# Query, key and value projections as half-precision products of high and low parts

## The reference

```python
def attention(q, k, v, ...):                     # q = layernorm(x), k = v = ctx
    Q = (q @ Wq.T + bq).reshape(16, 256, 16, 32)
    K = (k @ Wk.T + bk).reshape(16, 256, 16, 32)
    V = (v @ Wv.T + bv).reshape(16, 256, 16, 32)
    score = einsum('bshd,bsgd->bshg', Q, K)
    weight = softmax(score, axis=-1)
    return einsum('bshg,bsgd->bshd', weight, V).reshape(16, 256, 512) @ Wo.T + bo
x = x + attention(layernorm(x), ctx, ctx, ...)
x = x + ffn(layernorm(x))    # 8 experts of width 352, two per token, and a shared expert of width 704
```

## Time and profile before

| what | us |
|---|---|
| median of 3 runs | 1515.64 (1507.03 to 1521.95) |
| the profiled execution | 1513.93 |
| its span in the trace | 1512.2 |
| TensorE busy, weight loads busy | 1403.4, 1069.2 |
| VectorE, ScalarE, GpSimd busy | 906.3, 647.3, 502.0 |
| chain that ended last: TensorE's share | 80% |

### The profile page before, as it was taken

One profiled execution on the slowest core, in us unless ns is written; L12 is line 12 of the kernel. 1 busy time (PEld: TensorE's weight loads), 2 busy tenths in 40 slices (PEclk: granted clock), 3 DMA queues, 4 the chain that ended last, 5 costly groups with the idle time before them and its releaser, 6 DMA issues.

```text
span 1512.2 us, 33003 instructions
## 1 busy us (share of the span) xinstructions
PE 1403.4 (93%) x10387; PEld 1069.2 (71%) x10388; DVE 906.3 (60%) x1984; ACT 647.3 (43%) x1500; POOL 502.0 (33%) x607
## 2 busy tenths in 40 slices
PE   4489999999999999679989999999999999999997
PEld 4388888888888888556657765666666666666675
DVE  6388888888888888766776552222222222223666
ACT  4256656555665556541145442333333333332221
POOL 4234444444444443200567101111111111114554
PEclk9699999999999999889999999999999999999999
DMA  5456677666766775838724332222222222226997
GB/s 188 95 120 174 182 170 188 173 173 176 176 175 175 180 176 134 291 125 323 154 43 69 100 99 98 83 83 83 83 83 83 81 81 81 83 77 191 313 303 238
DMA packets 261893, 223.20 MB, mean 148 GB/s; under 512 B 182997, under 2 KB 191261, under 8 KB 261486
## 3 DMA queue, kind: packets, MB, share of 16 engines
q1 hardware_dynamic: 244488, 179.41, 42.2%
q0 software_dynamic: 12880, 35.47, 7.9%
q10 hardware_dynamic: 4470, 7.61, 1.6%
HBM read 129.30 MB, written 67.96 MB: 130 GB/s over the span
## 4 chain that ended last, share of the span: by engine, by line
PE 80%; DVE 6%; ACT 4%; SPq 3%; issue 3%; DMA 3%; POOL 1%; another core or an unknown queue 0%; ACTq 0%; DVEq 0%; POOLq 0%
PE psum_b L716 41%; PE psum_a L716 32%; PE psum_b L1032 2%; SPq L486 2%; PE psum_a L813 2%; PE psum_b L1054 2%; ACT spread_t L1100 1%; SPq L661 1%; PE psum_b L742 1%; DMA base_rows<-base 1%; DVE wdn L1797 1%; DMA heads<-in_wk_t 1%; DVE gate_act L1686 1%; ACT z_parts L1136 1%; DVE d_m L1711 1%
## 5 line engine op out<-in xcount | busy, mean ns | idle before, releaser
L716 PE MATMUL psum_a<-wgu,zg_t 128*128 x1704 | 269.0, 315 | 1.9 <-DVE zg_t L1808 1.7
L1947 POOL TENSOR_TENSOR spread<-pr,own 128x512 f32<-128x512 f32 x128 | 136.7, 1099 | 317.6 <-DVE pr L1463 306.6
L716 PEld LDWEIGHTS psum_a<-wgu,zg_t 128*128 128x128 f16 x1704 | 166.4, 98 | 91.1 <-issue 10.1
L2021 POOL DMA_INDIRECT zg<-z_rows,gather_ix x71 | 67.2, 946 | 431.2 <-DVE gather_ix L1804 423.9
L716 PE MATMUL psum_a<-zt_in,wsgu 128*128 128x256 f16 x1536 | 174.8, 277 | 5.8 <-DMA base<-x_rows 2.8
L716 PEld LDWEIGHTS psum_a<-zt_in,wsgu 128*128 128x128 f16 x1536 | 151.0, 99 | 31.7 <-issue 8.1
L1813 DVE SCALAR_TENSOR_TENSOR silu<-psum_a,w_scale,silu 128x352 f32<-128x352 f32 x71 | 41.5, 584 | 195.0 <-ACT silu L1302 195.0
L716 PE MATMUL psum_b<-wdn,act_t 128*128 (+1 forms) x639 | 149.6, 379 | 1.6 <-DVE act_t L1820 1.6
L716 PE MATMUL psum_b<-wsdn,sh_t 128*128 128x512 f16 (+1 forms) x576 | 131.8, 382 | 16.8 <-DVE sh_t L1692 14.1
L1302 ACT ACTIVATE silu<-psum_a,w_scale 128x352 f32<-128x352 f32 x71 | 39.3, 553 | 203.8 <-PE psum_a L716 203.8
L716 PEld LDWEIGHTS psum_b<-wsdn,sh_t 128*128 128x128 f16 (+1 forms) x576 | 53.9, 98 | 88.9 <-issue 16.0
(11 more groups left out here) (245 smaller groups left out, 2509.7 us busy)
## 6 DMA issues: line engine op xcount, KB each, us to landing
expert_rows<-y_sb SPq DMA_DIRECT2D x71, 256.0 KB
k_st<-k_parts SPq DMA_DIRECT2D x192, 64.0 KB, 2.2
q_st<-q_parts SPq DMA_DIRECT2D x192, 64.0 KB, 2.1
wgu_in<-in_wgu_t SPq DMA_DIRECT2D x8, 1408.0 KB, 18.2
x_sb<-in_x SPq DMA_DIRECT2D x16, 512.0 KB, 3.4
cx_in<-in_ctx_t SPq DMA_DIRECT2D x16, 512.0 KB, 6.7
x_res<-in_x SPq DMA_DIRECT2D x16, 512.0 KB, 5.3
value_rows<-heads SPq DMA_DIRECT2D x16, 512.0 KB, 6.2
```

Of the source, the lines that this page charges most:

```text
L716: return nc.tensor.matmul(o, l, r, start=start, stop=stop)
L1947: G.tensor_tensor(spread[:, u * UG:(u + 1) * UG, :].rearrange("p r (g t) -> p r g t", t=GT), pr[:, s, u * UG:(u + 1) * UG, :].unsqueeze(3) ...
L2021: pool.indirect_dma_start(out=zg[:, b, :], out_offset=None, in_=z_d[:, :], in_offset=bass.IndirectOffsetOnAxis(ap=gather_ix[:, b:b + 1], a ...
```

## The change

The three projections take half-precision operands. As these have a narrow range, every operand gets a power of two: xn a fixed one (2 to the 11th), each weight matrix one from its largest magnitude (`weight_scale`), and each block of the context one from its own largest magnitude, which `key_scale` now works out beside the scale of the keys. The outputs are scaled back where they leave PSUM. For this

- a second buffer `cx_w` takes the context for `weigh_context`, one pass ahead of the one for the products; SP loads it with one more DMA per pass (`load_cw`);
- `key_scale` writes to `k_next` and stands after `normalise_x`; in its old place stand the two instructions of `take_key_scale`, which copy it to `k_scale`;
- `split_context` on GpSimd waits for the context's scale (`c_scaled`) and has one more instruction, which scales the block in place;
- at the start the largest values are found, turned and used in three phases (`LIMITS`), each for one weight matrix; the low parts of wq and wv go from GpSimd to VectorE; the masks of `q_st` and `k_st` are written first on ScalarE;
- the first moves of keys stand ahead of the load of the third context block on SP's queue, and the first moves of queries are issued by ScalarE.

The output projection stays as it was. The diff, cut to its core:

```diff
         cx_in = sb("cx_in", [P, KC, BT], F32, early)
-        cx_t = sb("cx_t", [P, 2, KC, BT], F32R, early)
+        cx_w = sb("cx_w", [P, KC, BT], F32, early)
+        cx_t = sb("cx_t", [P, 2, KC, BT], F16, early)
...
-        wq = sb("wq", [P, 2, KC, D], F32R, one)
-        wk = sb("wk", [P, 2, KC, D], F32R, one)
-        wv = sb("wv", [P, 2, KC, D], F32R, one)
+        wq = sb("wq", [P, 2, KC, D], F16, one)
+        wk = sb("wk", [P, 2, KC, D], F16, one)
+        wv = sb("wv", [P, 2, KC, D], F16, one)
+        below_wo = sb("below_wo", [P, 3, KC, D], F32, one)
...
+            def load_cw(i):
+                sp.dma_start(cx_w[:, :, :], cx_v[:, :, bass.ds(i * BT, BT)]).then_inc(cw_loaded, 16)
...
             load_w(wk_in, wk_t, wk_loaded)
+            load_cw(1)
...
-            sp.wait_ge(cx_weighed, 1)
+            sp.wait_ge(cx_weighed, 2)
             load_cx(1)
+            load_cw(2)
+            move_keys(-1)
             sp.wait_ge(xn_ready, 2 * SUB)
             load_x(2)
+            sp.wait_ge(cx_weighed, 3)
+            load_cw(3)
+            store_values(-1)
             sp.wait_ge(cx_split, 2)
-            sp.wait_ge(cx_weighed, 2)
             load_cx(2)
...
+                if ahead3 and ahead4:
+                    sp.wait_ge(cx_weighed, i + 4)
+                    settle(sp)
+                    load_cw(i + 4)
                 if ahead3:
-                    sp.wait_ge(cx_weighed, i + 3)
-                    settle(sp)
                     sp.wait_ge(cx_split, i + 3)
                     settle(sp)
                     load_cx(i + 3)
...
+            def turn_limits(phase):
+                pe.wait_ge(limits_ready, phase + 1)
+                for n in range(*LIMITS[phase]):
+                    at = phase * BANK + (n - LIMITS[phase][0]) * P
+                    last = nc.tensor.transpose(psum_a[:, at:at + P], limit_rep[:, n, :], ident[:, :])
+                last.then_inc(limits_turned, 1)
+            turn_limits(0)
+            turn_limits(1)
+            pe.wait_ge(wk_split, 2)
             project_k(-1, range(KC))
-            pe.wait_ge(limits_ready, 1)
-            for n in range(4):
-                last = nc.tensor.transpose(psum_a[:, n * P:(n + 1) * P], limit_rep[:, n, :], ident[:, :])
-            last.then_inc(limits_turned, 1)
+            turn_limits(2)
             pe.wait_ge(wq_split, 1)
...
+                    nc.scalar.activation(xn_t[:, HI, :, s * P:(s + 1) * P], bank_ap(f"X{s}").rearrange("p (c t) -> p c t", c=KC),
+                                         ACT.Copy, scale=2.0 ** Z_EXP).then_inc(xt_high, 1)
...
-            weights_high(wk, wk_in, wk_loaded, 16)
-            x_out(-1)
-            weights_high(wq, wq_in, wq_loaded, 16)
-            weights_high(wv, wv_in, wv_loaded, 16)
-            weights_high(wo, wo_in, wo_loaded, 32)
-            keys_out(-1, 0)
-            keys_out(-1, 1)
-            queries_out(-1, 0)
-            queries_out(-1, 1)
+            def scaled_high(n, w, w_in, loaded, chunks):
+                act.wait_ge(loaded, 16)
+                act.wait_ge(w_scaled, n + 1)
+                nc.scalar.activation(w[:, HI, chunks], w_in[:, chunks], ACT.Copy, scale=w_power[:, 3 + n:4 + n]).then_inc(w_high, 1)
             act.wait_ge(const_ready, 1)
             copy8 = [q_st[3 * HD:ROWS], k_st[3 * HD:ROWS]]
             for rows_below, factor, size in ((copy8[0], ident[0:GT, 0:GT], MASK_Q), (copy8[1], other[:, :], 1.0)):
                 nc.scalar.activation(rows_below.rearrange("p j (h t) q -> p (j h) t q", t=GT), factor.unsqueeze(1).unsqueeze(3).broadcast_to([GT, NJ * H, GT, GI]),
                                      ACT.Copy, scale=size).then_inc(mask_ready, 1)
+            x_out(-1)
+            scaled_high(0, wk, wk_in, wk_loaded, slice(0, KC // 2))
+            scaled_high(0, wk, wk_in, wk_loaded, slice(KC // 2, KC))
+            scaled_high(1, wq, wq_in, wq_loaded, slice(0, KC))
+            scaled_high(2, wv, wv_in, wv_loaded, slice(0, KC))
+            keys_out(-1, 0)
+            keys_out(-1, 1)
+            queries_out(-1, 0)
+            queries_out(-1, 1)
+            act.wait_ge(q_low, 2)
+            for n, part in enumerate(PARTS_OF_Q):
+                for l in range(4):
+                    act.dma_start(q_st[HD * n:HD * (n + 1), :, HD * l:HD * (l + 1), :].rearrange("p j m g -> p j (m g)"),
+                                  q_parts[HD * l:HD * (l + 1), part].rearrange("p j c t -> p j (c t)")).then_inc(q_moved, 16)
+            weights_high(wo, wo_in, wo_loaded, 32)
...
-                    V.tensor_tensor(v_rows[:, s], bank_ap(f"V{s}"), bv_rep[:, :], ALU.add).then_inc(drained[BANK_OF[f"V{s}"]], 1)
+                    V.scalar_tensor_tensor(out=v_rows[:, s], in0=bank_ap(f"V{s}"), scalar=k_scale[:, 8:9], in1=bv_rep[:, :],
+                                           op0=ALU.mult, op1=ALU.add).then_inc(drained[BANK_OF[f"V{s}"]], 1)
...
             def weigh_context(n):
-                dve.wait_ge(cx_loaded, n * 16 + 16)
-                link(V.tensor_reduce(out=k_scale[:, 7:8], in_=cx_in[:, :, :].rearrange("p c t -> p (c t)"), axis=X, op=ALU.max, apply_absolute_value=True))
+                if isinstance(n, int) and n == 0:
+                    dve.wait_ge(cx_loaded, 16)
+                else:
+                    dve.wait_ge(cw_loaded, n * 16)
+                whole_block = cx_in if isinstance(n, int) and n == 0 else cx_w
+                link(V.tensor_reduce(out=k_bound[:, 2:3], in_=whole_block[:, :, :].rearrange("p c t -> p (c t)"), axis=X, op=ALU.max, apply_absolute_value=True))
                 dve.sem_inc(cx_weighed, 1)
             def spread_context():
-                V.tensor_copy(c_rep[:, :], k_scale[:, 7:8].broadcast_to([P, P])).then_inc(c_rep_ready, 1)
-            def key_scale(first=False):
-                bits = lambda n: k_scale[:, n:n + 1].bitcast(U32)
-                link(V.tensor_scalar(k_scale[:, 0:1], k_scale[:, 0:1], k_scale[:, 5:6], k_scale[:, 6:7], ALU.mult, ALU.add))
-                link(V.tensor_scalar(bits(1), bits(0), EXPONENT, None, ALU.bitwise_and))
-                link(V.tensor_scalar(bits(1), bits(1), float(SMALLEST << 23), None, ALU.max))
-                link(V.tensor_scalar(bits(2), bits(1), -1.0, float((2 * 127 + K_ROOM) << 23), ALU.mult, ALU.add))
-                if not first:
-                    link(V.tensor_copy(k_scale[:, 3:4], k_scale[:, 4:5]))
-                link(V.tensor_scalar(k_scale[:, 4:5], k_scale[:, 1:2], q_scale[:, 3:4], None, ALU.mult))
-                V.tensor_scalar(k_scale[:, 8:8 + KC], bias_col[:, 1, :], k_scale[:, 2:3], None, ALU.mult).then_inc(k_scaled, 1)
+                V.tensor_copy(c_rep[:, :], k_bound[:, 2:3].broadcast_to([P, P])).then_inc(c_rep_ready, 1)
+            def key_scale():
+                powers, ups = (k_next[:, n:n + 2].bitcast(U32) for n in (2, 4))
+                link(V.tensor_scalar(k_next[:, 0:1], k_next[:, 1:2], k_bound[:, 0:1], k_bound[:, 1:2], ALU.mult, ALU.add))
+                link(V.tensor_scalar(powers, k_next[:, 0:2].bitcast(U32), EXPONENT, None, ALU.bitwise_and))
+                link(V.tensor_scalar(powers, powers, float(SMALLEST << 23), None, ALU.max))
+                link(V.tensor_scalar(ups, powers, -1.0, float((2 * 127 + K_ROOM) << 23), ALU.mult, ALU.add))
+                mark(V.tensor_scalar(k_next[:, 10:10 + KC], bias_col[:, 1, :], k_next[:, 4:5], None, ALU.mult))
+                link(V.tensor_scalar(k_next[:, 7:9], w_power[:, 6:8], k_next[:, 3:4], None, ALU.mult))
+                link(V.tensor_scalar(k_next[:, 9:10], k_next[:, 7:8], k_next[:, 4:5], None, ALU.mult))
+                dve.sem_inc(c_scaled, 1)
             def bound_out(i):
                 wait_full(dve, "M0", i)
-                V.tensor_reduce(out=k_scale[:, 0:1], in_=bank_ap("M0")[:, 0:P], axis=X, op=ALU.max).then_inc(drained[BANK_OF["M0"]], 1)
+                V.tensor_reduce(out=k_next[:, 1:2], in_=bank_ap("M0")[:, 0:P], axis=X, op=ALU.max).then_inc(drained[BANK_OF["M0"]], 1)
             def next_key_scale(i):
                 wait_drained(dve, "M0", i)
+                dve.wait_ge(cx_split, i + 3)
                 key_scale()
-            def first_scales():
+            def take_key_scale():
+                link(V.tensor_scalar(k_bound[:, 3:4], k_scale[:, 2:3], q_scale[:, 3:4], None, ALU.mult))
+                V.tensor_copy(k_scale[:, 2:10 + KC], k_next[:, 2:10 + KC]).then_inc(k_scaled, 1)
+            def limits_out(phase):
+                first, end = LIMITS[phase]
+                dve.wait_ge(limits_turned, phase + 1)
+                link(V.tensor_reduce(out=limits[:, first:end], in_=psum_a[:, phase * BANK:phase * BANK + (end - first) * P].rearrange("p (n c) -> p n c", c=P),
+                                     axis=X, op=ALU.max))
...
-            def body(i, behind, ahead, ahead2, weighs=0):
+            def body(i, behind, ahead, ahead2, weighs=0, ahead3=True):
                 bound_out(i - 1)
                 if behind:
```

(65 more changed lines are left out.)

99 lines of the change are left out of this document (58 added, 41 removed).

## The result

The changed kernel takes 1581.96 us, the median of four runs (1580.5 to 1585.19). The kernel before takes 1515.8 us on the same chip (four runs). The ratio is 1.0444, with a 95% interval from 1.0411 to 1.0478: slower. The profiled execution has a span of 1581.3 us and a mean granted clock of 0.957.

What follows compares the result with a forecast made beforehand. TensorE was taken as nearly full, with VectorE's string up to z right behind as second bound. 1513.9 + 78 (13 passes) - 10.5 (start) = 1581.4, plus 1.7 for the median: 1583 us; range 1505 to 1602, likeliest case 1562 to 1602.

Steps and rivals of the forecast that it cites:

- The products: TensorE's projections in each attention pass: half-precision operands save 1.2 us a pass, between nothing and 1.7 us.
- Rival (c): Half-precision products gain nothing, staying at 123 ns; VectorE sets the pass, so still 1583 us; no case of its own.
- Two-column instructions wait for GpSimd: VectorE's late key scale: its two- and four-column instructions wait out GpSimd's four weight-spreading products, 2.8 us more a pass.
- the 16 ns: Four-column VectorE instruction takes 230 ns, one-column 214; the difference was read as a sign that such instructions wait for GpSimd.
- z late beyond its 0.8 us: VectorE's late key scale adds about 1.5 us ahead of z, whose first half has 0.8 us in hand: 0.7 us a pass.
- z halves held by the split: Later z meets GpSimd's context split; each half loses up to one GpSimd instruction, 1.1 us a pass counted.
- The clock: TensorE, idle waiting for z, drops to 1.2 GHz; the transposes behind slow, about 1.4 us a pass (0 to 1.9).
- A steady pass: Sum for one attention pass: 6.0 us longer, between 4.5 and 7.2; over 13 passes +78 us (58 to 94).
- The start: Before the first scores: earlier key and query moves bring 9.5 us, pass 0 another 1 us: -10.5 us (-6 to -13).
- the 2.2 us of landing: At the start, the last query move on ScalarE's queue was taken to land 2.2 us after its issue.
- (a): Rival: two- and four-column instructions don't wait for GpSimd; 1529 us, without z meeting the split 1514; chance 0.30.
- (b): Rival, faster: VectorE's string isn't late at the transposes of z, so TensorE's 1.2 us come through; 1490 us; chance 0.10.

Runs made afterwards that it cites:

- before_one_wide: The kernel before, with three idle linked one-column VectorE instructions added between the normalisation of x and the residual sums: 1525.99 us, ratio 1.0125.
- before_two_wide: The kernel before, with three idle linked two-column VectorE instructions added between the normalisation of x and the residual sums: 1582.56 us, ratio 1.0486.
- key_early: The changed kernel with the key scale calculation moved back to its old place, right behind `take_key_scale`: 1518.7 us, ratio 1.008 to the kernel before.
- key_after_values: The changed kernel with the key scale calculation moved behind VectorE's value step, after z: 1508.7 us, ratio 1.0011 to the kernel before.
- no_pool_scale: The changed kernel without GpSimd's instruction that scales the context (not the same computation): 1597.47 us, ratio 1.0627 to the kernel before.
- loads_held: The changed kernel with SP's next loads at the start held until the first 12 query moves have landed: 1573.01 us, ratio 1.0453 to the kernel before.
- key_single: The changed kernel with the late key scale worked out in 14 one-column instructions instead of 7, same place: 1557.16 us, ratio 1.0323 to the kernel before.

## Why the prediction was right

The time (1583 against 1582) and the sign came out, and the mechanism did too: before_one_wide and before_two_wide show that the two-column instructions wait for GpSimd's products, key_early and key_after_values that the calculation's place makes the loss. The match to 1 us is luck: two errors of some 7 us cancelled.

- **The products.** Priced at 1.2 us a pass (0 to 1.7). The step from pass 13 to pass 14, without the late key scale, is 1.37 us shorter than before: right. The parts: keys and queries take 10.6 us for 96 products instead of 12.0, from start to next start, 1.4 less; the value product 0.37 less by its record; and each group of four scores now takes 0.46 us to the next start (311.90 to 312.36) against 0.39, some 0.4 us a pass given back, which wasn't foreseen. Rival (c) is out.
- **Two-column instructions wait for GpSimd, +2.8 us.** Measured: 4.1 us for the calculation instead of the 1.5 reckoned without the wait, 2.6 us. The prediction let mask, mask, complement and bias go one per GpSimd instruction; it was the three on two columns, and the bias on four came when GpSimd was through, so no run shows whether four columns wait. That the 16 ns were read as a sign of the waiting form was an inference from thin evidence; before_one_wide and before_two_wide make it good for two columns. The Trainium skill's rule (SBUF — State Buffer, "Who interferes with whom") fits these three instructions; z beside GpSimd's scaling was not blocked to that instruction's end (0.73 us for a half, of a scaling of 2.86).
- **z late beyond its 0.8 us, +0.7 us.** The start of z moves by 4.69 us in the pass (35.27 us from the attention sums before it, against 30.58). That is 4.14 for the calculation, 0.66 for the normalisation of x, and 0.1 regained earlier. The 0.66 wasn't foreseen: the normalisation takes 1.82 us, not 1.16, since GpSimd's products now begin beside it. Of the 0.8 us in hand only 0.65 could be used, as TensorE starts 0.15 us after z's first half has ended. So the term is 0.85 instead of 0.7, and 0.55 more was missing from the sum. That VectorE would regain no more than 0.15 us at the early place was right: it waits 0.92 us for ScalarE ahead of the low part of xn.
- **z halves held by the split, +1.1 us.** Wrong: 0.2 us (0.73 against 0.54 for the first half, for which TensorE waits). The price of GpSimd's scaling was wrong too, 2.86 us instead of 1.05, above both bounds; and since this instruction is the one beside z and holds it only at its own start, the effect stayed small. It is real behind another neighbour: 1.7 us in no_pool_scale (2.90 against 1.19) and 2.0 in before_two_wide.
- **The clock, +1.4 us.** In the mean of the passes the stretch from the transposes of z to the attention sums is 1.3 us longer (5.7 against 4.4). In the pass shown it is only 0.7, though its transposes take 1.4 us more (1.94 and 2.44 against 1.04 and 1.91), as the wait behind them shrinks. Right in the mean, as the lower level of 1.2 GHz for part of the stretch.
- **A steady pass: 6.0 us predicted, 5.5 measured** (0.85 + 2.6 + 0.55 + 0.2 + 1.3), in place of 78 us 71.5.
- **The start, -10.5 us.** This is the step that failed. From the starts of the first scores of pass 1 (101.06 before, 97.96 after) it is -3.1 us. Pass 0 is 1 us shorter, as predicted (33.54 against 34.52 us); the first scores are 2.1 us earlier, not 9.5. The walk to the last issue was right within 1 us (55.73 against 54.8); the term that was mis-sized is the 2.2 us of landing, 8.55 in its place. The trace had a warning: before, with one queue, the last move landed within 2.1 us while nothing else was loading. The Trainium skill says it outright (DMA: Bandwidth & Descriptors, "Issuing engines are not separate DMA queues"): queues of different engines feed the same transfer engines, so that a second one saves issue time only. The runs agree: without loads beside the moves, two queues bring the scores 3.9 us earlier than one, as much as the last issue is earlier; with the loads beside them, nothing. And had the landing been 2.2 us, pass 0 would hardly have ended sooner: in loads_held, where the loads come later too, its attention sums come 0.7 us earlier and those of pass 1 0.7 us later.
- Past the attention stage the span is 2.1 us longer (904.5 against 902.4 us from the first scores of pass 15), with 3.12 us of waiting for value rows in the last pass; what brings that wait about wasn't tried.

So 6.5 us too much for 13 passes and some 7 us too much gain at the start met. Rivals (a) and (b) are decided against: the first by the 0.99 us of the two-column instructions, the second by TensorE's wait of 5.38 us for z. But the wait for GpSimd is only about half of the loss, 2.6 of 5.5 us a pass. Key_single, whose calculation has none of it, is still 3.2% slower than the kernel before, though 1 us a pass of that is its seven further instructions. The other half is the calculation's own time on the string to z, the longer normalisation of x and the clock.

## What to carry to other kernels

Where two engines are nearly full, a small calculation costs by its place. With the same seven instructions ahead of z the kernel is 4.4% slower than before, behind the value step it is level; look for a place where the neighbour is idle and nothing on the critical string stands behind it. When a wait is removed, name the next two waits before moving again: here z, the router's bank, the query moves and the context's split came up in turn within 1.5 us of each other. And a second queue was worth only the earlier issue here (3.9 us), and nothing with loads beside it; list what else is loading then, and what the next engine is still busy with.
